# ScalarE's order in the projection of a causal attention kernel: the casts of the next rows move ahead of a chunk's first two copies

## The chip, the cores and the metric

The kernel runs on one core of a Trainium2 chip, as one launch. The metric is the device time of the execution in microseconds, lower is better. A core has five engines that run side by side and meet only at semaphores: TensorE (PE, matrix products and transposes into PSUM), VectorE (DVE), ScalarE (ACT), GpSimd (POOL) and SyncE (SP, which issues the transfers here). Each engine carries out its own list of instructions in the order in which the program gives them.

## The reference, cut to what matters

The input x has shape 4 x 2048 x 256 in float32. What is computed:

```
h = layernorm(x)
q, k, v = h @ Wq, h @ Wk, h @ Wv          # 16 heads of 16
w = softmax(causal(q @ k.T * 0.25))
x = x + (w @ v) @ Wo + bo
h = layernorm(x)
# 8-bit feed-forward step: rows of h and columns of rhs are scaled by their
# largest magnitude, rounded to integers, multiplied, and scaled back
x = x + quantised_matmul(h, rhs)
```

The change lies in the first part, layernorm and the three projections. For accuracy a float32 value is carried there as two float16 values, a high part (the value cast to float16) and a low part (what is left), and a product of two such numbers is three float16 products: high by high, low by high and high by low.

## The kernel before, in words

The program has a projection, an attention and a last phase (output projection and feed-forward step). The projection goes over x in 16 chunks of 512 rows, numbered n = 0 to 15. For chunk n, in the order in which the data pass:

- SP loads the rows (line 567). DVE takes mean and variance (lines 652 and 659), ScalarE the square root (`root`, line 787), DVE the negated mean and the reciprocal (lines 664 and 665).
- POOL normalises the four tiles of 128 rows (line 611) and signals after the second and the fourth. In chunks 0 and 1 DVE does this.
- ScalarE casts two tiles at a time to the high part (`high_rows`, line 794), and POOL subtracts it from the rows for the low part (`low_rows`, line 623).
- PE transposes high and low parts, 16 blocks (line 854), and ScalarE copies them out of PSUM in two instructions (`take_xT`, line 801).
- PE makes the four 128 x 512 results of q and k (QK = 4, line 895), each of six products, in PSUM banks 0 to 3. For each of them ScalarE casts the high part out of PSUM (line 820), and DVE subtracts for the low part (`low_part`, line 681). SP stores both.
- PE makes v in two halves (line 912), in banks 2 and 3, and ScalarE copies them to the tile V (line 832).

The stages of two or three chunks are interleaved. While PE is at q and k of chunk n, the rows of chunk n + 1 are cast and given their low part; behind q and k of chunk n come the transposes of chunk n + 1, then v of chunk n. DVE takes the statistics of chunk n + 2 behind its fourth subtraction, the variance after its next reduction, and the negated mean and reciprocal after another; ScalarE's square root for chunk n + 2 stands between the two copies of v.

From chunk 2 on a further job is laid between these steps at fixed places, the row maxima of the first scores of attention, in turns. A turn is a pair of products on PE (lines 277, 282 and 263) into one of two pairs of banks, and one reduction on DVE (line 355, 1.2 us). PE's turn i waits until DVE has reduced turn i - 2. A chunk has six places, numbered 0 to 5: one behind each of the four results of q and k, one behind the transposes (4), one between the two halves of v (5). 68 turns are shared out over the 72 places of chunks 2 to 13, so a chunk has six or five of them; chunks 14 and 15 have an own share, with some places holding two.

All of this is an order written out by hand, one list for each engine. SP's list for chunk n is: the load of chunk n + 2, the stores of q, the stores of k; then for chunks 0 to 3 a wait until those stores have landed, and in chunks 0 to 7 eight loads of Q and K for attention.

Of the kernel before, what the change touches and what calls it, by code (L numbers as in the profile page):

```python
# [17 lines left out]
NC = B * NCH  # L18
# [463 lines left out]
def project(nc, x_t, Wq, Wk, Wv, qk_d, PS, identf, identh, maskid, mask, eps, scale, A, M, F):  # L482
    ctx = ExitStack()
    with ctx:
# [79 lines left out]
        @block.sync  # L564
        def _(sp):
            def load(n):
                sp.dma_start(xs[n % 2][:], x_t[n * CH:(n + 1) * CH, :]
                             .rearrange("(t p) d -> p t d", p=P)).then_inc(x_in[n % 2], 16)

            load(0)  # L570
            for t, src in zip(w, (Wq, Wk, Wv)):
                sp.dma_start(t[:], src.rearrange("(k p) n -> p k n", p=P)).then_inc(w_in, 16)
            load(1)
            for n in range(NC):
                b, c, s = n // NCH, n % NCH, n % 2
                if n + 2 < NC:
                    sp.wait_ge(xn_ready, 2 * n + 2)
                    load(n + 2)
                for i in range(2):
                    sp.wait_ge(lo_ready, n * QK + KC * (i + 1))  # L580
                    for p in range(2):
                        for o in range(KC):
                            heads = slice(b * H + o * (P // DH), b * H + (o + 1) * (P // DH))
                            sp.dma_start(qk_d[i][heads, p, :, c * CH:(c + 1) * CH],
                                         part[s][p][:, i * KC + o, :]).then_inc(stored[s], 16)
                    if n == COMBINE and i == 0:
                        max_rows(sp, A.Q, M, 0)
                if n < NCH:
                    if n == 0:
                        sp.wait_ge(fixed, 2)  # L590
                    sp.wait_ge(stored[s], (n // 2 + 1) * STORES)
                    load_attention(sp, A, qk_d, 0, n)
                elif n < 2 * NCH:
                    if n == NCH:
                        sp.wait_ge(fixed, 6)
                    load_attention(sp, A, qk_d, 1, 2 * NCH - 1 - n)
# [185 lines left out]
        @block.scalar  # L782
        def _(act):
            def root(n):
                s = n % 2
                act.wait_ge(var_ready, n + 1)
                nc.scalar.activation(std[s][:], mv[s][:, :, 1], ACT.Sqrt, bias=eps[:, 0:1]).then_inc(std_ready, 1)

            def high_rows(n, half):
                s, at = n % 2, slice(2 * half, 2 * half + 2)  # L790
                act.wait_ge(xn_ready, 2 * n + half + 1)
                if n >= 2 and half == 0:
                    act.wait_ge(tposed, n - 1)
                nc.scalar.copy(xp[s][:, 0, at, :], xn[s][:, at, :]).then_inc(xh_ready, 1)  # L794

            def take_xT(n):
                act.wait_ge(tposed, n + 1)
                if n >= 2:
                    act.wait_ge(v_ready, (n - 1) * KC)
                for i in range(2):  # L800
                    nc.scalar.copy(xT[n % 2][:, i].rearrange("p k t -> p (k t)"),  # L801
                                   PS[:, i, :].bitcast(F16)).then_inc(xT_ready, 1)

            root(0)
            for half in range(2):
                high_rows(0, half)
            root(1)
            take_xT(0)
            for half in range(2):
                high_rows(1, half)  # L810
            act.wait_ge(vT_back, 1)
            nc.scalar.copy(wp[2][:].rearrange("p i k c -> p (i k c)"),
                           PS[:, 7, :].bitcast(F16)).then_inc(wv_ready, 1)
            for n in range(NC):
                s = n % 2
                for j in range(QK):
                    act.wait_ge(qk_ready, n * QK + j + 1)
                    if n >= 2 and j == 0:
                        act.wait_ge(stored[s], n // 2 * STORES)
                    nc.scalar.copy(part[s][0][:, j], PS[:, j, :]).then_inc(hi_ready, 1)  # L820
                    if j % 2 == 1 and 2 <= n + 1 < NC:
                        high_rows(n + 1, j // 2)
                if n + 1 < NC:
                    take_xT(n + 1)
                else:

                    nc.scalar.preload_act_table_set("natural_log_exp_and_others")
                for j in range(KC):
                    if j == 1 and n + 2 < NC:
                        root(n + 2)  # L830
                    act.wait_ge(v_ready, n * KC + j + 1)
                    nc.scalar.copy(A.V[:, n * TPC + 2 * j:n * TPC + 2 * j + 2, 0:H * VS]
                                   .rearrange("p t (h e) -> p t h e", e=VS)[:, :, :, 0:DH],
                                   PS[:, 2 + j, :].rearrange("p (t h d) -> p t h d", h=H, d=DH)
                                   ).then_inc(v_taken, 1)
# [725 lines left out]
```

## Time and profile before

| | us |
|---|---|
| median of 3 runs | 1688.85 (1688.56 to 1699.98) |
| the profiled execution | 1689.07 |
| its span | 1687.3 |
| busy in the span: PE, DVE, ACT, POOL | 1568.8, 1522.1, 1361.9, 290.6 |
| projection: from the start to the first score product | 249.7 |
| granted clock of TensorE, mean | 0.976 |

The span is the time from the first to the last instruction that the profiler saw. A granted clock of 1.00 means 2.4 GHz, 0.50 means 1.2 GHz. Busy times of an engine are sums over its instructions; an engine that is waiting for a semaphore is not busy.

### The profile page before, as it was taken

How to read it: one execution, taken by the hardware profiler on the slowest of the kernel's cores; microseconds unless marked ns; L12 is line 12 of the kernel's file. 1: busy time of each engine (PE TensorE's matmuls, PEld its weight loads, DVE VectorE, ACT ScalarE, POOL GpSimd, SP SyncE). 2: the span in 40 equal slices, each digit the busy share in tenths (PEclk: the TensorE clock that was granted, in tenths of full speed). 3: DMA queues.
4: the chain of work that ended last, by engine and by line, in shares of the span. 5: the costliest groups of instructions: out<-in, count | busy, mean ns of one | idle time of the engine just before them, and what ended most of it. 6: DMA issues, size and time to landing. Idle time of an engine off the chain costs nothing.

```text
span 1687.3 us, 40684 instructions
## 1 busy us (share of the span) xinstructions
PE 1568.8 (93%) x16715; PEld 627.1 (37%) x16715; DVE 1522.1 (90%) x1839; ACT 1361.9 (81%) x2659; POOL 290.6 (17%) x397
## 2 busy tenths in 40 slices
PE   4788889999999999999999999999999999999965
PEld 2444443333333333333333333333333333344433
DVE  5577779999999999999999999999999999678876
ACT  3444448999999999999999999999999999877641
POOL 5433310201020202111111111111102020100120
PEclk9899999999999999999999999999999999999986
DMA  2444320111121212121212112121112142034532
GB/s 81 142 146 138 113 88 12 37 36 40 32 79 37 73 37 68 43 63 43 62 49 56 58 48 59 46 60 46 59 46 68 47 115 88 15 107 139 155 109 77
DMA packets 105614, 118.79 MB, mean 70 GB/s; under 512 B 20689, under 2 KB 87509, under 8 KB 105429
## 3 DMA queue, kind: packets, MB, share of 16 engines
q1 hardware_dynamic: 105428, 116.19, 23.9%
q8 instruction: 132, 2.16, 0.6%
q14 instruction: 54, 0.43, 0.1%
HBM read 66.81 MB, written 48.76 MB: 68 GB/s over the span
## 4 chain that ended last, share of the span: by engine, by line
DVE 54%; PE 27%; DMA 1%; issue 1%; ACT 1%; SPq 1%; POOL 0%; ACTq 0%; DVEq 0%
DVE pmax L355 46%; PE psum L1155 12%; PE psum L1136 6%; DVE pblk L355 4%; PE psum L263 3%; PE psum L1196 3%; PE psum L282 2%; PE psum L277 2%; DMA f_rs<-inverse_sums 1%; DVE V L1438 1%; DVE V L1457 1%; DVE V L1445 1%; ACT prob L1326 1%; PE psum L1220 1%; DVE f_amax L1463 1%
## 5 line engine op out<-in xcount | busy, mean ns | idle before, releaser
L1326 ACT ACTIVATE prob<-psum 128x512 f32<-128x512 f32 (+1 forms) x2304 | 1181.0, 574 | 138.0 <-PE psum L1136 114.6
L355 DVE TENSOR_REDUCE pmax<-psum 128x2 f32<-128x1024 f32 (+1 forms) x960 | 1101.1, 1216 | 16.7 <-PE psum L282 10.1
L1155 PE MATMUL psum<-prob,V 128*32 128x256 f32 x8704 | 676.0, 391 | 0.0
L1136 PE MATMUL psum<-Q,K 50*128 50x512 f16 (+3 forms) x2560 | 465.3, 350 | 3.8 <-ACT prob L1326 1.0
L1392 POOL TENSOR_SCALAR_AFFINE_SELECT prob<-prob 128x512 f32<-128x512 f32 x256 | 160.3, 639 | 1178.4 <-ACT prob L1326 1175.9
L263 PE MATMUL psum<-K,Q 48*128 48x512 f16 x1536 | 298.6, 385 | 12.5 <-DVE pmax L355 12.5
L1155 PEld LDWEIGHTS psum<-prob,V 128*32 128x32 f32 x8704 | 181.5, 108 | 294.1 <-issue 214.0
L1136 PEld LDWEIGHTS psum<-Q,K 50*128 50x128 f16 x2560 | 174.6, 94 | 251.9 <-ACT prob L1326 184.4
L263 PEld LDWEIGHTS psum<-K,Q 48*128 48x128 f16 x1536 | 74.3, 93 | 257.4 <-DVE pmax L355 208.7
L355 DVE TENSOR_REDUCE pblk<-psum 128x8 f32<-128x1024 f32 x128 | 151.8, 1219 | 6.5 <-PE psum L282 6.3
L282 PE MATMUL psum<-K,Q 48*128 48x512 f16 (+3 forms) x1024 | 129.5, 300 | 0.0
L277 PE MATMUL psum<-mask,maskid 64*128 64x128 bf16 (+2 forms) x1280 | 104.2, 231 | 9.3 <-DVE pmax L355 5.3
L277 PEld LDWEIGHTS psum<-mask,maskid 64*128 64x128 bf16 x1280 | 58.5, 95 | 57.0 <-DVE pmax L355 35.0
L820 ACT CAST part<-psum 128x512 f16<-128x512 f32 x64 | 37.2, 587 | 50.7 <-PE psum L895 50.6
L1196 PE MATMUL psum<-f_wo,f_us 128*128 128x256 f32 x256 | 74.9, 421 | 0.0
L681 DVE TENSOR_TENSOR part<-psum,part 128x512 f16<-128x512 f32 x64 | 43.6, 687 | 29.1 <-ACT part L820 28.8
L801 ACT COPY f_rs<-psum 128x1024 f16<-128x1024 f16 x32 | 30.8, 1014 | 36.4 <-PE psum L854 36.4
L895 PE MATMUL psum<-f_rs,wpq 128*128 128x512 f16 x192 | 47.7, 392 | 5.9 <-ACT f_rs L801 5.9
L1196 PEld LDWEIGHTS psum<-f_wo,f_us 128*128 128x128 f32 x256 | 46.4, 199 | 17.6 <-issue 12.7
L912 PE MATMUL psum<-wpv,f_rs 128*128 128x256 f16 x384 | 52.8, 294 | 0.0
L623 POOL TENSOR_TENSOR f_us<-f_x,f_us 128x512 f16<-128x512 f32 x32 | 36.9, 1155 | 79.9 <-ACT f_us L794 79.9
L282 PEld LDWEIGHTS psum<-K,Q 48*128 48x128 f16 x1024 | 48.7, 95 | 0.5
(122 smaller groups left out, 723.7 us busy)
## 6 DMA issues: line engine op xcount, KB each, us to landing
f_x<-in_L_attn_x SPq DMA_DIRECT2D x32, 512.0 KB, 4.0
unnormalised<-ust SPq DMA_DIRECT2D x64, 256.0 KB, 3.1
q_parts<-part SPq DMA_DIRECT2D x64, 128.0 KB
k_parts<-part SPq DMA_DIRECT2D x64, 128.0 KB
Q<-q_parts SPq DMA_DIRECT2D x128, 64.0 KB, 2.4
K<-k_parts SPq DMA_DIRECT2D x128, 64.0 KB, 2.1
out<-V SPq DMA_DIRECT2D x16, 512.0 KB, 3.4
f_rs<-inverse_sums SPq DMA_DIRECT2D x28, 256.0 KB
```

What stands on the lines that cost most here:

```text
L263: return nc.tensor.matmul(bank, Q[p][rows, pair, qt * P:(qt + 1) * P], K[p][rows, pair, kc * CH:(kc + 1) * CH], start=True, stop=True)
L277: nc.tensor.matmul(to, maskid[at:at + HALF, i, :], mk, start=i == 0, stop=False, skip_group_check=True)
L282: m = nc.tensor.matmul(bank[:, col:col + n], Q[p][rows, pair, qt * P:(qt + 1) * P], K[p][rows, pair, a * CH:a * CH + n], start=False, stop ...
L355: nc.vector.tensor_reduce(to, of, axis=AX.X, op=ALU.max).then_inc(M.mx_free, 1)
L681: nc.vector.tensor_tensor(part[s][1][:, j], PS[:, j, :], part[s][0][:, j], ALU.subtract).then_inc(lo_ready, 1)
L895: m = nc.tensor.matmul(PS[:, j, :], wp[i][:, of_w, k, o * P:(o + 1) * P], xT[s][:, of_x, k, :], start=(of_w, of_x, k) == (0, 0, 0), stop=( ...
L912: m = nc.tensor.matmul(PS[:, 2 + j, (t % 2) * D:(t % 2 + 1) * D], xT[s][:, of_x, k, t * P:(t + 1) * P], wp[2][:, of_w, k, :], start=(of_w, ...
L1136: m = nc.tensor.matmul(PS[:, SB + i % RING, at:at + n], K[it % 2][rows, pair, kb * P:(kb + 1) * P], Q[it % 2][rows, pair, (c + 1) * CH - n ...
L1155: m = nc.tensor.matmul(PS[32 * h:32 * h + 32, UB, to:to + n], V[:, it // NG * NT + kb, col:col + 32], prob[(it * NSTEP + k) % PRING][:, h, ...
L1196: m = nc.tensor.matmul(bank[:, q % 2 * D:(q % 2 + 1) * D], us[j % 4][:, o, q * P:(q + 1) * P], wo[:, o, :], start=False, stop=o == KC - 1, ...
L1326: nc.scalar.activation(prob[g % PRING][:, h, 0:n], PS[:, SB + i % RING, 0:n], ACT.Exp, scale=by).then_inc(exp_done, 1)
L1392: nc.gpsimd.affine_select(out=d, in_=d, compare_op=ALU.is_ge, fill=0.0, base=0, pattern=[[0, G], [1, P]], channel_multiplier=-1).then_inc( ...
```

## The change

ScalarE's list for the q and k results of a chunk is changed. Before, the cast of the first two tiles of chunk n + 1 stands behind the second cast out of PSUM, and that of the last two tiles behind the fourth. After, they stand ahead of the first and ahead of the second, and ahead of the waits of those casts. The condition covers the same chunks (n + 1 from 2 to 15).

```
                 for j in range(QK):
+                    if j < 2 <= n + 1 < NC:
+                        high_rows(n + 1, j)
                     act.wait_ge(qk_ready, n * QK + j + 1)
                     if n >= 2 and j == 0:
                         act.wait_ge(stored[s], n // 2 * STORES)
                     nc.scalar.copy(part[s][0][:, j], PS[:, j, :]).then_inc(hi_ready, 1)
-                    if j % 2 == 1 and 2 <= n + 1 < NC:
-                        high_rows(n + 1, j // 2)
```

`high_rows(n, half)` waits for POOL's normalisation of that half (`xn_ready`), and for its first half until the transposes two chunks earlier are done (`tposed`).

## Rows read from the trace of the kernel before

**Rows 1.** The page: the chain that ended last, by engine.
```profile
DVE 54%; PE 27%; DMA 1%; issue 1%; ACT 1%; SPq 1%; POOL 0%; ACTq 0%; DVEq 0%
```

**Rows 2.** Busy time by stretch, columns as headed.
```profile
core 0: us, PE busy (x) PEld busy (x) DVE busy (x) ACT busy (x) POOL busy (x), PEclk, DMA share, GB/s
...
400.00:800.00 400.00, 393.79 (x4653) 141.71 (x4653) 391.24 (x372) 372.26 (x731) 60.50 (x85) 1.00 0.20 53
193.80:207.30 13.50, 11.39 (x79) 5.80 (x78) 11.13 (x21) 6.58 (x11) 4.55 (x7) 1.00 0.39 121
```

**Rows 3.** Timeline, PE, first score products: start, duration, work [idle before, releaser].
```profile
249.72 0.59 PE L1136 MATMUL psum<-Q,K 50*128 50x512 f16 x3 [0.93 <-PEq L484]
```

**Rows 4.** Waits between 66 and 232 us: total us, times, longest.
```profile
PE psum L854 <- POOL f_us L623: 24.7, 12, 2.1
```

**Rows 5.** Timeline of PE in chunk 12.
```profile
193.84 1.46 PE L895 MATMUL psum<-f_rs,wpq 128*128 128x512 f16 x6
...
202.90 1.07 PE L854 MATMUL psum<-identh,f_us 128*128 128x128 f16 x16 [2.11 <-POOL f_us L623]
...
205.64 0.39 PE L263 MATMUL psum<-K,Q 48*128 48x512 f16 x2
...
207.28 1.46 PE L895 MATMUL psum<-f_rs,wpq 128*128 128x512 f16 x6
```

**Rows 6.** Timeline of DVE in chunk 12.
```profile
203.06 1.21 DVE L355 TENSOR_REDUCE pmax<-psum 128x2 f32<-128x1024 f32 x1
...
204.47 1.19 DVE L355 TENSOR_REDUCE pmax<-psum 128x2 f32<-128x1024 f32 x1
206.65 0.17 DVE L664 TENSOR_SCALAR nmean<-mv 128x4 f32<-128x4 f32 x1 [0.98 <-ACT std L787]
206.73 0.17 DVE L665 RECIPROCAL rstd<-std 128x4 f32<-128x4 f32 x1
...
209.39 0.69 DVE L681 TENSOR_TENSOR part<-psum,part 128x512 f16<-128x512 f32 x1 [1.39 <-ACT part L820]
```

**Rows 7.** Timeline of POOL in chunk 12.
```profile
201.69 1.16 POOL L623 TENSOR_TENSOR f_us<-f_x,f_us 128x512 f16<-128x512 f32 x1 [2.29 <-ACT f_us L794]
207.00 2.17 POOL L611 TENSOR_SCALAR f_x<-f_x,nmean,rstd 128x256 f32<-128x256 f32 x4 [4.16 <-DVE rstd L665]
```

**Rows 8.** Timeline of ScalarE in chunk 12.
```profile
200.99 0.62 ACT L794 CAST f_us<-f_x 128x512 f16<-128x512 f32 x1
...
208.78 0.59 ACT L820 CAST part<-psum 128x512 f16<-128x512 f32 x1 [0.71 <-PE psum L895]
```

**Rows 9.** Timeline, all engines, chunks 1 and 2.
```profile
46.11 4.07 PE L912 MATMUL psum<-wpv,f_rs 128*128 128x256 f16 x24
...
52.28 0.30 ACT L787 ACTIVATE std<-mv,eps 128x4 f32<-128x4 f32 x1 [2.79 <-DVE mv L659]
52.48 0.57 ACT L832 COPY V<-psum 128x512 f32<-128x512 f32 x1
...
59.68 0.42 SPq L567 DMA_DIRECT2D f_x<-in_L_attn_x  x1
...
63.50 1.41 DVE L652 BATCH_NORM_STATS2 stats<-f_x 128x6 f32<-128x256 f32 x4 [5.19 <-DMA f_x<-in_L_attn_x]
```

**Rows 10.** Timeline, all engines, chunks 3 and 4.
```profile
78.93 1.21 DVE L355 TENSOR_REDUCE pblk<-psum 128x8 f32<-128x1024 f32 x1
...
84.90 1.46 PE L895 MATMUL psum<-f_rs,wpq 128*128 128x512 f16 x6
...
86.67 0.43 SPq L567 DMA_DIRECT2D f_x<-in_L_attn_x  x1
...
92.81 1.39 DVE L652 BATCH_NORM_STATS2 stats<-f_x 128x6 f32<-128x256 f32 x4
```

**Rows 11.** Busy time by stretch, one microsecond in chunk 8, columns as in rows 2.
```profile
149.00:150.00 1.00, 1.00 (x6) 0.39 (x5) 0.37 (x3) 0.78 (x1) 0.00 (x0) 0.50 0.54 182
```

**Rows 12.** Timeline of PE in chunk 8.
```profile
147.48 1.70 PE L854 MATMUL psum<-identh,f_us 128*128 128x128 f16 x16 [2.10 <-POOL f_us L623]
...
151.77 0.39 PE L263 MATMUL psum<-K,Q 48*128 48x512 f16 x2
```

More of the change, by code:

```diff
@@ L816, in _ @@
                 for j in range(QK):
+                    if j < 2 <= n + 1 < NC:
+                        high_rows(n + 1, j)
                     act.wait_ge(qk_ready, n * QK + j + 1)
@@ L820, in _ @@
                     nc.scalar.copy(part[s][0][:, j], PS[:, j, :]).then_inc(hi_ready, 1)
-                    if j % 2 == 1 and 2 <= n + 1 < NC:
-                        high_rows(n + 1, j // 2)
                 if n + 1 < NC:
```

## The prediction

> **What bounds the kernel now.** I read the busy lines and the chain of waits first, then the busy time by stage, then the waits of the projection, then one of its chunks engine by engine. The chain of the whole run is DVE over PE [rows 1]. By stage: in attention PE is busy 393.79 of 400 us and DVE 391.24, and nothing that ScalarE's projection code does is in it; in a projection chunk PE is busy 11.39 of 13.50 us and DVE 11.13 [rows 2]. So only the stretch up to the first score product at 249.72 us [rows 3] can change, and what it saves moves the rest forward one for one as long as the projection's last chunk keeps its shape.
>
> In the projection one wait of PE stands out: the transposes of the next rows wait for POOL's low parts, 12 times and 24.7 us between 66 and 232 us, 2.06 us each, once in each of chunks 3 to 14 [rows 4]. Chunk 12 shows how. It lasts from PE's first product at 193.84 to the next chunk's at 207.28, 13.44 us. PE idles 2.11 us before the transposes [rows 5]. They wait for POOL's second low part, which ends at 202.85 [rows 7] and starts when ScalarE's second high part ends at 201.61 [rows 8]. That cast was queued behind the fourth cast of the chunk. Its input had been ready for about 5 us: POOL's normalisation takes 2.17 us and for the chunk after it starts at 207.00, before that chunk's first product [rows 5, 7].
>
> **The change, step by step.** No instruction is added or removed. 28 casts of 0.62 us (the two high parts of each of chunks 2 to 15) change place within ScalarE's order; SP's and POOL's own orders, the DMAs and their sizes stay. ScalarE is busy 6.6 us of a chunk, so their time costs nothing; what counts is what each now waits for and what is queued behind it.
>
> *Step 1, the old wait goes.* With both high parts made ahead of the chunk's second cast, POOL's two low parts of 1.16 us are done less than 3 us behind them, long before PE is through with its fourth product. PE's 2.11 us go entirely, in chunks 3 to 14.
>
> *Step 2, what is late next.* PE then issues the transposes 2.11 us sooner, and the row-maximum turn behind them, and the first value product. The next turn (the row at 205.64) reuses the bank of the turn two before it, which DVE reduces at 203.06 to 204.27 [rows 6]. Freed of the old wait PE would be there at 203.53, so it waits 0.78 us for DVE. From there to the next chunk's first product is 1.64 us (205.64 to 207.28). So the new length is 204.27 + 0.04 + 1.64 - 193.84 = 12.11 us, 1.33 less.
>
> *Step 3, the wait that the change adds.* The first high part now stands ahead of the first cast. DVE's fifth reduction ends at 205.66 [rows 6]; the mean and reciprocal no longer wait 0.98 us for ScalarE, whose square root comes earlier, so the reciprocal starts near 205.67, POOL 0.27 us later at 205.94, half its rows are done 1.1 us after that, at 207.04, and the high part runs about 207.09 to 207.6 (two such instructions back to back are spaced 0.5 us). The first product of the new chunk starts at 205.95 and the cast could follow it by 1.50 us (208.78 less 207.28) [rows 5, 8], at 207.45. So the cast is 0.14 us late. The second high part has its input at 208.1, while the first cast ends; the second cast is not touched. Behind the late cast stand DVE's first subtraction and all of DVE's chunk, so I take 0.15 us per chunk. Bounds: 0 if POOL's first half comes 0.15 us sooner; 1.75 us as in chunk 2, where POOL's rows would come that late after the cast's old place. Chunk 12's rows are nearest, and I take theirs. Net per chunk 1.2 us.
>
> The Trainium skill ("TensorE: Matmul & The Clock Gate", architectural detail, engine queue depths) says that ScalarE's and VectorE's queues are strictly first in, first out, which speaks against the change: no cast passes a high part that waits. The trace agrees: a copy whose product had ended at 50.18 started at 52.48, behind a square root that waited 2.79 us for DVE [rows 9]. Were it otherwise, the 0.15 us of nine chunks would be saved too and the sum be 1.4 us larger.
>
> *Step 4, the chunks that differ.* Chunks 1 and 2: nothing gained. Chunk 1's square root waits for rows loaded from memory, and in chunk 2 the load that was issued at 59.68 ends DVE's wait of 5.19 us at 63.50 [rows 9]. That issue hangs on stores and loads of earlier chunks in SP's order. The casts of chunk 2 do become up to 2.5 us later (the first from about 53 to 54.7), but DVE would finish the fourth subtraction about 60.5, 3 us before those rows land; this cover is what that cost rests on. Chunk 3: the reduction at 78.93 ends at 80.14; 1.68 us behind it the next first product is at 81.8, now 84.90 [rows 10]: 3.1 us, half of it clock (step 5). Chunk 4: its statistics would come at 89.9, now 92.81, but the load at 86.67 lands 3.8 to 4.1 us later, at about 90.65 [rows 9, 10]: 0.75 of the 1.2 us is lost, 0.45 left. Chunks 5 to 13: 9 x 1.2 = 10.8 us. Chunk 14 has its turns laid differently, with DVE idle between them, so nothing takes the wait's place: 2.0 us.
>
> *Step 5, the clock.* After the wait in chunk 8 the granted clock is 0.50, the 1.2 GHz level, against 1.00, 2.4 GHz, in the rest [rows 2, 11]. From transposes to the turn behind the first value product that costs 151.77 - 147.48 = 4.29 us against 205.64 - 202.90 = 2.74 at full clock [rows 5, 12]: 1.5 us. Chunks 3 and 14 show the same loss, and in all three PE had just stood idle 1.9 to 2.1 us. The other chunks had the same wait without a fall, so the fall is not certain to go with it; with PE's idle down to 0.8 us I take it to go. Chunk 3's is in its 3.1; chunks 8 and 14 give 3.0.
>
> Sum: 3.1 + 0.45 + 10.8 + 2.0 + 3.0 = 19.35 us. The profiled execution took 1689.07 us (span 1687.3), 0.22 above the median of 1688.85. So 1669.7 us.
>
> **The rivals.**
> - *The waits go, the falls of the clock stay* (other idle stretches set them off, as 11 waits gave only three falls): 4.5 us less gain, 1674.3. For it: no row links a fall to its idle alone. 0.18.
> - *The row loads become the bound while chunks also load Q and K* (chunks 4 to 8). For it: the 0.75 us in chunk 4. Against: from chunk 5 on stores and loads move forward with the chunk, and statistics come some 2 us behind the landing. If those five gain nothing, 0.45 + 4 x 1.2 + 1.5 = 6.8 us are lost: 1676.5. 0.15.
> - *PE alone sets the chunk*: the 0.78 us of step 2 don't arise and all 12 waits come back: 12 x 2.06 + 4.5 = 29 us, 1660. Against: DVE has 13.44 - 0.98 - 1.39 = 11.07 us of work in a chunk of 11.33, in a fixed order with PE. 0.05.
> - *Slower: POOL's normalisation is the new wait of each chunk.* The place is the first high part, ahead of the first cast. If it holds that cast 1.75 us, as in chunk 2, eleven chunks cost 0.42 us more each than the 1.33 saved: +4.6, 1693.7 where chunk 14 and the clock bring nothing. It decides from 1.33 us of delay on; step 3 finds 0.14. 0.07.
> - *Nothing arrives*: the projection's last stores, or the start of attention, hold the end where it is. Then 1689. Against: they hang on the last chunk's casts, which move forward. 0.05.
>
> **How the numbers follow.** The forecast has 0.50, with 1667 to 1673. The range from 1664 to 1681 takes in the two rivals below it in gain and leaves out 0.17. A measurement of this kernel tells 1% (16.9 us, below 1672) from no change. Most of the forecast's own part lies under 1672, and the PE rival too: faster 0.53. The other rivals are within 1%: 0.45. Slower by over 1% needs 1.33 + 16.9/11 = 2.9 us of delay in every chunk: 0.02.
>
> **What would show it.** Step 1: no PE wait for POOL's low part. Step 2: chunk 12 lasts 12.3 us and PE waits under 1 us for a reduction ahead of the second value product. Step 3: the first cast starts 1.6 to 1.7 us behind the chunk's first product, not 1.50, and DVE idles about 1.3 us ahead of its first subtraction and nowhere else. Step 4: chunk 3 starts near 69.4 as before; DVE waits for a load in chunk 4. Step 5: clock 1.00 from chunk 3 to 15. Attention starts near 230 us. It would be wrong if the first cast is held by over 0.5 us, or if the fall of the clock comes back at other places.

## The result

The changed kernel takes 1673.38 us (median of four runs, 1668.7 to 1674.36), against 1691.3 us before (four runs, 1688.56 to 1699.98). The ratio is 0.988, 95% interval 0.9837 to 0.9922. In a second session it was 1671.19 against 1693.34 us, ratio 0.9871 (0.9836 to 0.9905). The forecast was 1669.7 us in a range of 1664 to 1681. By the profiled executions, from which the forecast was worked out, the kernel is 15.7 us faster (1673.34 against 1689.07), where 19.35 were forecast.

The waits of the changed kernel between 66 and 232 us, which answer to [rows 4]. Columns: total us, times, longest.

```profile
PE psum L263 <- DVE pmax L355: 9.3, 11, 1.4
...
PE psum L277 <- DVE pmax L355: 4.2, 2, 3.7
ACT f_us L794 <- POOL f_x L611: 3.0, 10, 0.3
...
DVE stats L652 <- DMA f_x<-in_L_attn_x: 0.4, 1, 0.4
```

PE's 12 waits for POOL's low parts are gone from the list. In their place PE waits for DVE's reductions, ScalarE's high part waits ten times 0.3 us for POOL's normalisation, and DVE waits once for a load. Chunk 12 on PE, answering to [rows 5] (it now starts at 180.84):

```profile
180.84 1.46 PE L895 MATMUL psum<-f_rs,wpq 128*128 128x512 f16 x6
...
187.72 1.07 PE L854 MATMUL psum<-identh,f_us 128*128 128x128 f16 x16
...
191.43 0.39 PE L263 MATMUL psum<-K,Q 48*128 48x512 f16 x2 [0.90 <-DVE pmax L355]
...
193.08 1.46 PE L895 MATMUL psum<-f_rs,wpq 128*128 128x512 f16 x6
```

It lasts 12.24 us. The transposes start 6.88 us into the chunk, with no wait; the turn ahead of the second value product waits 0.90 us. DVE, ScalarE and POOL around the end of the same chunk, answering to [rows 6], [rows 8] and [rows 7]:

```profile
190.17 1.21 DVE L355 TENSOR_REDUCE pmax<-psum 128x2 f32<-128x1024 f32 x1
191.29 0.37 DVE L659 BATCH_NORM_AGGREGATE mv<-stats 128x2 f32<-128x6 f32 x4
191.58 1.19 DVE L355 TENSOR_REDUCE pmax<-psum 128x2 f32<-128x1024 f32 x1
192.69 0.16 DVE L664 TENSOR_SCALAR nmean<-mv 128x4 f32<-128x4 f32 x1
192.75 0.17 DVE L665 RECIPROCAL rstd<-std 128x4 f32<-128x4 f32 x1
192.84 1.20 DVE L355 TENSOR_REDUCE pmax<-psum 128x2 f32<-128x1024 f32 x1
195.30 0.69 DVE L681 TENSOR_TENSOR part<-psum,part 128x512 f16<-128x512 f32 x1 [1.26 <-ACT part L822]
```

```profile
193.28 0.59 ACT L832 COPY V<-psum 128x512 f32<-128x512 f32 x1 [1.29 <-PE psum L912]
194.16 0.62 ACT L794 CAST f_us<-f_x 128x512 f16<-128x512 f32 x1 [0.29 <-POOL f_x L611]
194.68 0.58 ACT L822 CAST part<-psum 128x512 f16<-128x512 f32 x1
```

```profile
193.03 2.17 POOL L611 TENSOR_SCALAR f_x<-f_x,nmean,rstd 128x256 f32<-128x256 f32 x4 [7.83 <-DVE rstd L665]
```

The reduction that frees PE's bank ends at 191.38 and PE goes on at 191.43. ScalarE is free 0.29 us before POOL has the first half ready. The first cast starts at 194.68, 1.60 us behind the chunk's first product at 193.08, where it was 1.50 before. DVE idles 1.26 us, ahead of its first subtraction and nowhere else in the chunk.

Attention starts with the first score product, answering to [rows 3]:

```profile
231.49 0.59 PE L1136 MATMUL psum<-Q,K 50*128 50x512 f16 x3 [0.93 <-PEq L484]
```

That is 18.23 us earlier. Where they come from, by the start of each chunk's first product (before, after):

| stretch | before | after | difference | forecast |
|---|---|---|---|---|
| chunk 0 | 12.98 | 12.99 | 0.0 | 0 |
| chunks 1 and 2 | 12.95 + 19.35 | 8.90 + 24.03 | +0.6 | 0 |
| chunk 3 | 15.54 | 13.66 | -1.9 | -3.1 |
| chunk 4 | 13.44 | 12.71 | -0.7 | -0.45 |
| chunks 5 to 13 | 122.38 | 109.07 | -13.3 | -12.3 with the clock of chunk 8 |
| chunk 14 | 14.64 | 11.82 | -2.8 | -3.5 |
| chunk 15 | 14.36 | 14.36 | 0.0 | 0 |

The first chunk's first product itself starts 0.13 us earlier.

Chunk 14 gained 0.7 us less than forecast. PE's wait of 2.01 us for the low parts is gone there, but a new one of 0.77 us has come, for DVE's row maxima (`mparts`). Two small instructions of DVE ahead of them last longer than before, L311 0.35 us in place of 0.17, and this one (before, then after), while POOL makes the low parts that now come at this time:

```profile
224.21 0.20 DVE L316 TENSOR_SCALAR mparts<-negm 128x64 f16<-128x64 f32 x1
```

```profile
209.09 0.64 DVE L316 TENSOR_SCALAR mparts<-negm 128x64 f16<-128x64 f32 x1
```

```profile
207.40 2.27 POOL L623 TENSOR_TENSOR f_us<-f_x,f_us 128x512 f16<-128x512 f32 x2
```

```profile
210.13 0.22 PE L293 MATMUL psum<-identh,mparts 128*128 128x128 f16 x1 [0.77 <-DVE mparts L318]
```

The remaining 2.4 us of difference between the score product and the end (18.23 us there, 15.8 in the span) are lost at the tail. Attention is not it: DVE's first addition of the residual in the last phase is at 1476.81 before and 1458.75 after, still 18.06 us apart, and so are the first ten of its sixteen additions to 0.01 us; the last one is at 1663.58 and 1647.83, 15.75 apart. Ahead of that last one stands this, first of before, then of after (timeline of PE, the output projection of the last rows):

```profile
1658.65 2.55 PE L1196 MATMUL psum<-f_wo,f_us 128*128 128x256 f32 x8
```

```profile
1641.38 3.78 PE L1196 MATMUL psum<-f_wo,f_us 128*128 128x256 f32 x8
```

The same eight products take 1.2 us more. Busy time by stretch of the changed kernel, columns as in [rows 2], has the granted clock at 0.50 there, 1.2 GHz:

```profile
1640.00:1645.00 5.00, 5.00 (x14) 2.93 (x12) 4.45 (x9) 1.71 (x4) 0.00 (x0) 0.50 0.00 0
```

It is not a property of the change: the same kernel profiled in the second session has its first score product at 229.51 and a span of 1665.6 us, so 1436.1 us from there to the end, against 1440.0 here and 1437.6 before. Those two profiles of one kernel are 2.1 us apart at the first ten additions and 5.9 at the last, although the eight products above take 3.78 us in both.

### The profile page after: what moved, and what is told of

Its sections match the earlier page's. It is cut to its first block, busy times and chain, and to the rows that moved or that the text cites. A ratio compares the mean times of both kernels' runs of the same rounds, so it can differ in the third digit from the quotient of the medians.

```text
span 1671.5 us, 40684 instructions
## 1 busy us (share of the span) xinstructions
PE 1565.0 (94%) x16715; PEld 624.0 (37%) x16715; DVE 1521.1 (91%) x1839; ACT 1363.3 (82%) x2659; POOL 290.7 (17%) x397
## 4 chain that ended last, share of the span: by engine, by line
DVE 54%; PE 28%; DMA 1%; ACT 1%; issue 1%; SPq 1%; POOL 0%; ACTq 0%; DVEq 0%
DVE pmax L355 46%; PE psum L1155 12%; PE psum L1136 6%; DVE pblk L355 4%; PE psum L263 3%; PE psum L1196 3%; PE psum L282 2%; PE psum L277 2%; DMA f_rs<-inverse_sums 1%; DVE V L1438 1%; ACT prob L1326 1%; DVE V L1457 1%; DVE V L1445 1%; PE psum L1220 1%; DVE f_amax L1463 1%
## 5 line engine op out<-in xcount | busy, mean ns | idle before, releaser
L912 PE MATMUL psum<-wpv,f_rs 128*128 128x256 f16 x384 | 49.1, 280 | 0.0
L895 PE MATMUL psum<-f_rs,wpk 128*128 128x512 f16 x192 | 46.6, 380 | 1.8 <-ACT V L832 1.8
L611 POOL TENSOR_SCALAR f_x<-f_x,nmean,rstd 128x256 f32<-128x256 f32 x56 | 30.4, 558 | 100.8 <-DVE rstd L665 97.4
```

The source lines that it names most:

```text
L895: m = nc.tensor.matmul(PS[:, j, :], wp[i][:, of_w, k, o * P:(o + 1) * P], xT[s][:, of_x, k, :], start=(of_w, of_x, k) == (0, 0, 0), stop=( ...
L912: m = nc.tensor.matmul(PS[:, 2 + j, (t % 2) * D:(t % 2 + 1) * D], xT[s][:, of_x, k, t * P:(t + 1) * P], wp[2][:, of_w, k, :], start=(of_w, ...
```

## The experiments

**One half undone.** The first half's high part stays early, the second half's goes back.

```
                 for j in range(QK):
-                    if j < 2 <= n + 1 < NC:
-                        high_rows(n + 1, j)
+                    if j == 0 and 2 <= n + 1 < NC:
+                        high_rows(n + 1, 0)
                     ...
                     nc.scalar.copy(part[s][0][:, j], PS[:, j, :]).then_inc(hi_ready, 1)
+                    if j == 3 and 2 <= n + 1 < NC:
+                        high_rows(n + 1, 1)
```

> Half of the change undone: the first half's high part stays ahead of the first cast, the second half's goes back behind the fourth. Theory (PE waits for the second low part alone): the wait of 2.1 us is back in every chunk, chunk 12 of 13.4 to 13.5 us, first score product near 249. Rival (each half carries half of the gain): chunk 12 near 12.8, first score product near 240.

Measured: 1690.68 us (the kernel before on the same chip 1696.32, one run each), first score product at 249.91 us. Its waits between 66 and 249 us:

```profile
PE psum L856 <- POOL f_us L623: 24.7, 12, 2.1
```

The waits are back to the tenth of a microsecond of [rows 4], and so is each chunk's length to 0.2 us (13.43 in chunk 12). So the early first half alone brings nothing. It costs nothing either: POOL has the rows ready in time here, and the first cast of chunk 12 starts 1.49 us behind the first product, as before. Its trace also bears on the clock. Chunk 8, timeline of PE and then busy time by stretch:

```profile
147.63 1.82 PE L856 MATMUL psum<-identh,f_us 128*128 128x128 f16 x16 [2.11 <-POOL f_us L623]
...
151.93 0.39 PE L263 MATMUL psum<-K,Q 48*128 48x512 f16 x2
```

```profile
149.00:150.00 1.00, 1.00 (x8) 0.37 (x6) 0.28 (x4) 0.51 (x1) 0.00 (x0) 0.50 0.52 171
```

Of the twelve chunks from 3 to 14 the clock falls after the waits of the same three as before, 3, 8 and 14 [rows 11, 12]; in chunks 1 and 2 it also falls in both kernels. In none of the nine traces without that wait does it fall in chunk 8.

**Both halves at the second cast.** The smallest edit that could do it.

```
                     nc.scalar.copy(part[s][0][:, j], PS[:, j, :]).then_inc(hi_ready, 1)
-                    if j % 2 == 1 and 2 <= n + 1 < NC:
-                        high_rows(n + 1, j // 2)
+                    if j == 1 and 2 <= n + 1 < NC:
+                        high_rows(n + 1, 0)
+                        high_rows(n + 1, 1)
```

(against the kernel before)

> Both high parts behind the second cast: the first half at its old place, the second half moved up to it. Theory: POOL's second low part ends about 6.8 us behind the chunk's first product, just before PE wants it at 6.95, so the whole gain is there with the smallest edit: chunk 12 of 12.1 to 12.2 us, first score product 230 to 231. Rival (the early first half is needed): PE still waits 0.5 us and more for POOL.

Measured: first score product at 231.25 us, chunk 12 of 12.12 us, 1674.01 us in all (one run; before on the same chip 1696.32). POOL in chunk 12, which starts at 181.29:

```profile
181.25 2.18 POOL L611 TENSOR_SCALAR f_x<-f_x,nmean,rstd 128x256 f32<-128x256 f32 x4 [5.40 <-DVE rstd L665]
185.70 2.27 POOL L623 TENSOR_TENSOR f_us<-f_x,f_us 128x512 f16<-128x512 f32 x2 [2.27 <-ACT f_us L794]
```

The low parts end at 187.97, 6.68 us into the chunk, and PE takes them at 188.17 without a wait. So the gain of the change is all in the second half coming two casts earlier.

**Both behind the casts.** The high parts of the change, but each behind its cast.

```
-                    if j < 2 <= n + 1 < NC:
-                        high_rows(n + 1, j)
                     ...
                     nc.scalar.copy(part[s][0][:, j], PS[:, j, :]).then_inc(hi_ready, 1)
+                    if j < 2 <= n + 1 < NC:
+                        high_rows(n + 1, j)
```

> Both high parts early, but behind the first and second cast in place of ahead of them. Theory (the change adds a wait of 0.14 us on POOL ahead of the first cast, and takes PE's 2.1 us wait away by the place of the second half): no wait for POOL's low part, the first cast 1.50 us behind the chunk's first product, chunk 12 of 12.1 us in place of 12.23, first score product 1.0 to 1.5 us earlier than in the changed kernel, near 230.2. Rival (being ahead of the casts is what matters): PE's wait comes back in part and the first score product is later than 232.

Measured: chunk 12 of 12.13 us, 0.1 less than with the change, and the first cast 1.50 us behind the first product (181.97 behind 180.47), as expected. But the first score product comes at 231.67 and not near 230.2: chunk 2 took 24.18 us and chunk 14 12.58, against 24.03 and 11.82 in the changed kernel and 22.59 and 11.81 in its second profile. In chunk 14 PE waits 1.53 us for DVE's maxima, where it waits 0.77 with the change. In total 1672.09 us against 1671.19 for the changed kernel on the same chip: no difference that counts. The price of the added wait is 0.1 us in four chunks (7, 10, 12 and 13) and 0.01 or less in the other five from 5 to 13; the expectation of the whole missed.

**Both ahead of the first cast.** It asks for the slower rival's mechanism: how much does it cost when POOL really holds the first cast?

```
-                    if j < 2 <= n + 1 < NC:
-                        high_rows(n + 1, j)
+                    if j == 0 and 2 <= n + 1 < NC:
+                        high_rows(n + 1, 0)
+                        high_rows(n + 1, 1)
```

> Both high parts ahead of the first cast. Theory (the loop through POOL sets the chunk as soon as the first cast waits for POOL): the loop now holds POOL's whole normalisation, 1.07 us more, so 12.26 + 1.07 = 13.3 us for chunk 12, first cast about 2.6 us behind the first product, first score product near 242, though PE has no wait for POOL's low parts. Rival (the moved wait is covered by DVE's idle time): chunk 12 stays below 12.5 us.

Measured: chunk 12 of 13.31 us, first score product at 238.66 and not near 242 (chunks 5, 8 and 11 take 12.2 to 12.35 us), 1680.85 us (one run; before on the same chip 1696.32). ScalarE in chunk 12, which starts at 185.20:

```profile
185.40 0.59 ACT L833 COPY V<-psum 128x512 f32<-128x512 f32 x1 [1.28 <-PE psum L913]
186.28 0.62 ACT L794 CAST f_us<-f_x 128x512 f16<-128x512 f32 x1 [0.30 <-POOL f_x L611]
187.36 0.62 ACT L794 CAST f_us<-f_x 128x512 f16<-128x512 f32 x1 [0.46 <-POOL f_x L611]
187.89 1.12 ACT L823 CAST part<-psum 128x512 f16<-128x512 f32 x2
```

The first cast is 2.69 us behind the first product, and the chunk is 1.07 us longer than with the change, which is the 1.1 us of POOL's second half. PE has no wait for POOL's low parts and still gains almost nothing in such a chunk: a loop that runs DVE, POOL, ScalarE, DVE sets it.

**The statistics behind the fourth reduction**, first with the change as it is.

```
                 low_part(n, 3)
+                turns(n, 3)
                 if n + 2 < NC:
                     statistics(n + 2)
-                turns(n, 3)
```

> The changed kernel, with DVE's statistics of the rows after next moved behind its fourth reduction, so that this reduction comes 1.3 us sooner and frees PE's bank. Theory (beside PE's wait for that reduction there is a loop of the same length: DVE's first subtraction to its fifth reduction 9.7 us, then reciprocal, POOL's half normalisation, high part, first cast, 2.55 us, 12.26 in all): PE's wait for the reduction ahead of the second value product goes, but chunk 12 stays at 12.2 to 12.3 us, the first cast is 2.4 us behind the first product, and the first score product stays within 1 us of 231.5. Rival (PE's wait for the reduction is the only limit): chunk 12 of 11.4 to 11.5 us, first score product near 223.

Measured: chunk 12 of 12.37 us, 1670.77 us in all against 1671.19: nothing gained. PE in that chunk:

```profile
182.50 0.39 PE L263 MATMUL psum<-K,Q 48*128 48x512 f16 x2 [0.63 <-DVE pmax L355]
...
185.96 0.39 PE L263 MATMUL psum<-K,Q 48*128 48x512 f16 x2 [0.34 <-DVE pmax L355]
...
187.70 0.39 PE L263 MATMUL psum<-K,Q 48*128 48x512 f16 x2
```

The wait ahead of the second value product is gone, and 0.97 us of waits have come up at two earlier turns; the first cast is now 3.04 us behind the first product (expected: 2.4). DVE works without a pause from its first subtraction at 180.62 to the reciprocal at 190.45, POOL starts at 190.72, the high part at 191.85 and the first cast at 192.38, each behind the one before. So the loop is real and as long as the chunk, and PE's wait for the fourth reduction was one of two limits at the same height. That the whole gains nothing is in part chance: chunk 3 starts at 66.26 us, 2.3 to 3.6 us sooner than in the two profiles of the changed kernel, and chunk 14 takes 14.71 us in place of 11.82. There PE waits for DVE's maxima, and the granted clock, in the third column from the end, is at 0.50 from 208 to 211 us:

```profile
207.96 0.26 PE L293 MATMUL psum<-identh,mparts 128*128 128x128 f16 x1 [2.20 <-DVE mparts L318]
```

```profile
208.00:211.00 3.00, 3.00 (x13) 1.00 (x13) 1.15 (x3) 0.18 (x1) 0.00 (x0) 0.50 0.22 63
```

**The same with the high parts behind the casts**, which opens the loop as well.

> Both high parts behind the first and second cast, and the statistics behind the fourth reduction. Theory: this opens the loop through POOL and the wait for the reduction both; then PE's own work sets the chunk, 11.3 to 11.4 us, DVE idles 0.3 us in it, and the first score product is near 222 (10 chunks of 0.8 us less than with the parts behind the casts alone), total near 0.984 of the kernel before. Rival (rows loaded from memory arrive too late in chunks 4 to 8 once chunks are shorter): DVE waits for loads of 0.5 us and more in those chunks, first score product near 226.

Its edit, against the changed kernel, is the diff of *both behind the casts* and the diff of the statistics together. Measured: chunk 12 of 11.27 us, first score product at 219.61, 1661.52 us (1659.33 to 1666.99), ratio to the kernel before 0.9823 (0.9785 to 0.9862). DVE and PE around the end of chunk 12, which goes from 170.13 to 181.40:

```profile
182.16 1.20 DVE L355 TENSOR_REDUCE pmax<-psum 128x2 f32<-128x1024 f32 x1
183.51 0.69 DVE L681 TENSOR_TENSOR part<-psum,part 128x512 f16<-128x512 f32 x1 [0.15 <-ACT part L820]
```

```profile
179.75 0.39 PE L263 MATMUL psum<-K,Q 48*128 48x512 f16 x2
180.08 1.48 PE L912 MATMUL psum<-wpv,f_rs 128*128 128x256 f16 x12
181.40 1.46 PE L895 MATMUL psum<-f_rs,wpq 128*128 128x512 f16 x6
```

Neither engine waits for more than 0.16 us: the chunk is PE's own work, with DVE 0.15 us behind. Half of the 12 us that it gains over the high parts behind the casts alone (231.67 to 219.61) come from chunk 2: the reduction now stands ahead of the statistics that wait for loaded rows, and chunk 3 starts at 64.09 and not at 70.23. Rows do arrive late in chunks 3 and 4 (DVE waits 1.96 and 1.64 us), as the rival said, and chunks 3 to 5 are the long ones, 13.37, 12.34 and 12.70 us.

**The loads earlier in SP's order.** Rows n + 3 are loaded behind the stores of chunk n.

```
-                if n + 2 < NC:
-                    sp.wait_ge(xn_ready, 2 * n + 2)
-                    load(n + 2)
+                if n == 0:
+                    sp.wait_ge(xn_ready, 2)
+                    load(2)
                 for i in range(2):
                     ...
+                if n + 3 < NC:
+                    sp.wait_ge(xn_ready, 2 * n + 4)
+                    load(n + 3)
                 if n < NCH:
```

> The changed kernel, and SP issues the load of rows n + 3 behind the stores of chunk n, ahead of its wait for those stores and of the loads of Q and K. Theory (chunks 1 and 2 gained nothing because the next rows' load held DVE, which hid the late casts): DVE's waits for loaded rows go, POOL's normalisation in chunk 2 starts right behind its fill of K near 49.5 in place of 52.5, the first product of chunk 3 comes 6 to 8 us earlier, near 62.5, DVE's 0.4 us in chunk 4 go too, and the first score product is near 223. Rival (stores and loads of Q and K hold these chunks in another way): chunk 3 starts at 68 or later and the total stays within 2 us of the changed kernel.

Measured: chunk 3 starts at 61.70 us (69.87 with the change, 68.54 in its second profile), first score product at 225.41, 1666.93 us (1665.59 to 1669.04), ratio 0.9844 (0.9807 to 0.9882). ScalarE and POOL in chunk 2, the chunk's first product being at 46.01:

```profile
46.66 0.57 ACT L835 COPY V<-psum 128x512 f32<-128x512 f32 x1
50.89 0.62 ACT L797 CAST f_us<-f_x 128x512 f16<-128x512 f32 x1 [3.66 <-POOL f_x L614]
51.41 0.58 ACT L825 CAST part<-psum 128x512 f16<-128x512 f32 x1
```

```profile
42.49 7.06 POOL L606 MEMSET K<- 32x4096 f16 x2
49.76 2.17 POOL L614 TENSOR_SCALAR f_x<-f_x,nmean,rstd 128x256 f32<-128x256 f32 x4 [0.20 <-POOL K L606]
```

With the load out of the way the next cover shows: ScalarE holds the first cast 3.66 us for POOL, which is filling the constant rows of K until 49.55. While it fills, DVE's negated mean and reciprocal, which POOL also needs, take 2.80 and 2.72 us where [rows 6] has 0.17; they end at 49.58. The expectation that DVE's waits for rows would go in chunk 4 and later was wrong: of 4.3 us in four waits, three with 3.5 us lie behind 65 us. The load issued at 91.35 us was followed at once by eight loads of Q and K, and its rows were there at 97.74, 6.4 us later, where the load of [rows 9] took 3.8 us. Chunk 5 took 14.40 us for it.

**All three together.**

> All three together: high parts behind the first and second cast, statistics behind the fourth reduction, early loads. Theory: chunks 4 to 13 at PE's own 11.3 us or less, chunk 3 from near 60, first score product near 214, total near 0.980 of the kernel before. Rival (the loads were hidden once the statistics come later): first score product stays near 219.6.

Measured: 1660.72 us (1656.64 to 1661.92), ratio 0.9796 (0.9758 to 0.9834), first score product at 217.60. It has the lowest median of all that ran, but by 0.8 us over the one without the early loads (on another chip, each against its own runs of before), which is not more than their spread. Chunk 3 starts at 59.29, as expected near 60; chunk 6 takes 15.49 us, with DVE waiting 2.93 us for rows, PE 2.39 us for DVE, and the clock at 0.50 behind it (from 101 to 104 us), and more than half of the 4.8 us by which chunk 3 starts earlier than without the early loads is given back.

## Why the prediction was right

*Step 1* held: PE's 12 waits are gone. The half undone and the two halves at the second cast show that they hung on the second half alone.

*Step 2* held: PE's next wait is the fourth reduction, 0.90 us (forecast 0.78, to which the chunk's shift by 0.1 us adds), and from the end of that reduction to the next chunk is 1.70 us (1.68).

*Step 3* held: chunk 12 was forecast at 12.26 us and is 12.24. The delay of the first cast is 0.10 us, not 0.14. It costs only four of the nine chunks 5 to 13 anything, as the high parts behind the casts show. What the step did not say is that this small delay was the end of a loop with no slack in those chunks: with both halves ahead of the first cast chunk 12 grew by the full 1.07 us. The slower rival named the right place, and where it put the point from which the change loses, 1.33 us of delay, the experiment with 1.09 us more delay than the change, 1.2 us in all, stands just short of it: 13.31 us a chunk against 13.44 before. What kept it from happening is that POOL starts its normalisation at the chunk's first product (193.03 and 193.08), as worked out.

*Step 4*, chunks 1 and 2: the sum held, but not as "nothing gained" in each. Chunk 1 gained 4.1 us, since PE's wait of 2.43 us for POOL goes there too, and the low clock behind it (the value products of [rows 9] take 2.78 us and not 4.07); chunk 2 lost 4.7, since the rows still land at the same time. The cover was named rightly. DVE's wait for the load in chunk 2 is 3.88 us where it was 5.19 [rows 9], and with the loads issued earlier chunk 3 starts 6.8 to 8.2 us sooner. That the late casts cost nothing only under this cover is borne out there: ScalarE then waits 3.66 us for POOL, and PE 2.58 us for the DVE reduction that stands behind it. Chunk 4's wait for rows is 0.37 us where 0.75 was forecast. Chunks 5 to 13 gained 13.3 and not 12.3, since I had taken chunk 12 for all: chunks 5 and 9, with most of the turns that have mask products (line 277), gained 1.5 us each, 6 and 11 gained 1.3, chunk 8 2.9 with its clock, and the other four 1.2. Chunk 14 was put at 2.0 us besides the clock because "nothing takes the wait's place"; a wait of 0.77 us for DVE's maxima does.

*Step 5* held for chunks 8 and 14 and failed for chunk 3. The clock stays at 1.00 from chunk 4 to 15, but in chunk 2 PE now waits for DVE twice, 3.7 us each time, and it is the lower level that chunk 3 starts at. Busy time by stretch, clock in the third column from the end:

```profile
58.00:62.00 4.00, 4.00 (x39) 2.76 (x34) 2.00 (x3) 1.93 (x2) 0.00 (x0) 0.58 0.33 85
65.00:72.00 7.00, 5.53 (x25) 2.97 (x26) 4.07 (x10) 1.40 (x3) 2.87 (x5) 0.53 0.38 127
```

The first product group of chunk 3 takes 2.65 us in place of 1.46. This is the 1.2 us by which chunk 3's term was too large. In the second profile of the same kernel the clock is back at 70 us, the group takes 1.92 us, and the chunk 12.94. At the start of attention the clock is at the lower level in both kernels, equally long (253.5 to 260.4 us before, 236.1 to 242.9 after).

The rest of the difference to the forecast (19.35 forecast, 18.23 in the projection, 15.7 in the time) is the last phase: from the first score product to the end two profiles of one kernel differ by 3.9 us, 3.8 of them in its last six additions. The forecast took what the projection saves to move the rest forward one for one; that held up to the last phase and not through it. The last rows' products at the lower clock explain 1.2 us of the 2.4 against the kernel before; the rest I did not trace.

Of the rivals, the one on loads was right in kind (one wait of 0.37 us with the change, 3.6 us in chunks 3 and 4 once most chunks take 11.3 us) and far too dear at 6.8 us. The one on the clock speaks of 11 waits; by [rows 4] they are 12. The falls behind them went with them; where a wait of over 2 us came up elsewhere, a fall came with it (chunk 14 with the statistics moved, chunk 6 with all three). PE alone as the limit, named at 0.05, is reached only after both DVE's order and the place of the high parts are changed.

**What stays open.** The medians of the kernel before are 1691 to 1694 us, with runs up to 1699.98, and the changed kernel's are 1671 to 1673: a gap of 18 to 22 us by medians, against 15.7 by the two profiled executions. In the seven runs of before in the second session the mean granted clock mostly goes with the time: 1688.97 us at 0.980, 1699.59 at 0.972 (an exception is 1690.63 at 0.975). The changed kernel's four there are at 0.979 to 0.982. So the slower runs of before may have more falls of the clock behind PE's 2.1 us waits, and the change may save more in those; there is no trace of one, and it stays a guess.

## What to carry to other kernels

Before moving an instruction ahead on an engine in order, write down the time at which its input is ready and the time at which the engine would otherwise take up what is behind it; here they were 0.1 us apart for the first half, and the move paid since the second half reached POOL two casts earlier. When a wait of an engine is removed, look for the next one by the bank or buffer that it will want, and then for a loop of the same length: two limits at the same height hide each other: in chunk 12 removing either alone gave 12.13 and 12.37 us against 12.24, and removing both 11.27. Put an instruction that may wait behind the one whose result others need, if both places are early enough for its own reader.

## What the runs showed that was not expected

- The clock falls behind PE's waits repeat: two kernels with the same waits (the one before and the one with a half undone) fall to 1.2 GHz in the same chunks, 3, 8 and 14, out of twelve equal waits of 1.9 to 2.1 us. In these the fall comes 0.1 to 0.9 us after the transposes behind the wait have begun. No transposes are needed for it: in chunk 14 with the statistics moved the fall comes at the end of a wait of 2.20 us for DVE, and in chunk 6 of all three together 0.7 us behind a wait of 2.39 us, in products of q. Why three of twelve waits have a fall and nine have none stays open.
- Small instructions of DVE can last longer while POOL works. In chunk 14 L311 and L316 take 0.17 and 0.20 us before and with both halves at the second cast, where POOL is idle, but 0.35 and 0.64 with the change and 1.04 and 0.81 with the high parts behind the casts, where POOL makes low parts at that time; with early loads the reciprocal took 2.72 us beside POOL's fill of K. Each of the longer ones ends 0.03 to 0.06 us behind the end of the POOL instruction that runs beside it. DVE's reductions of 1.2 us and its subtractions keep their length beside POOL. So these small ones wait for POOL or share something with it; no run was made to tell which.
- Moving a load ahead of eight smaller ones helped in chunks 1 and 2, where DVE's waits for rows went from 6.28 and 3.88 us to 0.80 and none, and not in chunk 5: 6.4 us from issue to rows where 3.8 us was measured when the eight stood ahead of it, with the DMA engines' share at 0.61 to 0.76.
- A wait of PE for DVE costs more where DVE stands behind a load: in the changed kernel PE waits 3.7 us twice in chunk 2 for reductions behind late casts and late rows. Moving one reduction ahead of the statistics brought chunk 3 forward by 6.1 us where the high parts stand behind the casts, and by 2.3 to 3.6 us with the change as it is.
